# Units of 88 slots in place of 96 in the expert FFN of the second layer

## The reference, cut to what matters

```python
x = _layernorm(x).reshape(-1, 256)                       # 1024 rows
probs = softmax(x @ gate_w)                              # 64 experts
top_vals, top_idx = jax.lax.top_k(probs, 8)
rw = scatter(top_vals / sum(top_vals), top_idx)          # 1024 x 64, 8 per row
g = einsum('th,ehi->tei', x, w_gate)                     # 256 -> 96
u = einsum('th,ehi->tei', x, w_up)
h = silu(g) * u * rw[:, :, None]
out = einsum('tei,eih->th', h, w_down)                   # 96 -> 256
```

## Time and profile before

| what | value |
|---|---|
| time, median of 3 runs | 365.51 us (364.02 to 365.74) |
| the profiled execution's own time | 366.64 us |
| its span, first to last instruction | 364.9 us |
| mean granted TensorE clock | 0.894 |
| PE busy | 271.3 us (74%) |
| DVE busy | 242.4 us (66%) |
| POOL busy | 157.3 us (43%) |
| ACT busy | 148.4 us (41%) |
| moved by DMA | 89.63 MB, mean 246 GB/s |

### The profile page before, as it was taken

One profiled execution on the slowest core, in us unless ns is written; L12 is line 12 of the kernel. 1 busy time (PEld: TensorE's weight loads), 2 busy tenths in 40 slices (PEclk: granted clock), 3 DMA queues, 4 the chain that ended last, 5 costly groups with the idle time before them and its releaser, 6 DMA issues.

```text
span 364.9 us, 6915 instructions
## 1 busy us (share of the span) xinstructions
PE 271.3 (74%) x1993; PEld 225.5 (62%) x1993; DVE 242.4 (66%) x885; ACT 148.4 (41%) x427; POOL 157.3 (43%) x195
## 2 busy tenths in 40 slices
PE   4898428803775016637899999979999999998852
PEld 1334218702775015526788988968888988886741
DVE  0699999898947845435668997968677776441001
ACT  2145624430664335212444444434444444446700
POOL 4552020300242787777777100000777753337770
PEclk9999999965599555785999999999999999998988
DMA  4899999962890133349999999956999999965532
GB/s 112 297 305 320 286 348 361 332 212 61 252 272 18 70 113 110 112 166 295 372 385 384 379 282 320 345 192 175 265 327 319 331 335 336 316 203 173 170 102 73
DMA packets 46789, 89.63 MB, mean 246 GB/s; under 512 B 8384, under 2 KB 12320, under 8 KB 46752
## 3 DMA queue, kind: packets, MB, share of 16 engines
q10 hardware_dynamic: 20400, 37.95, 32.3%
q1 hardware_dynamic: 20208, 34.45, 29.6%
q0 software_dynamic: 6144, 16.79, 14.3%
HBM read 51.91 MB, written 37.26 MB: 244 GB/s over the span
## 4 chain that ended last, share of the span: by engine, by line
PE 53%; DVE 22%; POOL 11%; issue 5%; DMA 3%; ACT 2%; SPq 1%; POOLq 0%; DVEq 0%; ACTq 0%
PE psum L854 23%; PE psum L862 15%; POOL expert_rows L586 8%; DVE work L1192 6%; PE psum L842 6%; DVE top L1188 5%; PE psum L743 3%; DVE stats L1163 2%; PE psum L732 2%; PE psum L921 2%; POOL xn L645 1%; PE psum L669 1%; POOL rstd L555 1%; DVE xs L1217 1%; POOL pen L645 1%
## 5 line engine op out<-in xcount | busy, mean ns | idle before, releaser
L586 POOL DMA_INDIRECT expert_rows<-x_rows,place_at x64 | 62.7, 979 | 24.5 <-issue 24.5
L1089 ACT ACTIVATE up<-psum 96x96 f32<-96x96 f32 x128 | 31.5, 246 | 80.1 <-PE psum L854 80.1
L1474 DVE TENSOR_TENSOR up<-up,psum 96x96 f32<-96x96 f32 x128 | 32.0, 250 | 39.5 <-ACT up L1089 31.9
L619 POOL DMA_INDIRECT work<-expert_rows,gather_at x32 | 30.3, 947 | 63.5 <-issue 56.1
L1469 DVE COPY silu<-psum 128x192 f32<-128x192 f32 x128 | 45.6, 357 | 16.4 <-PE psum L842 11.4
L842 PEld LDWEIGHTS psum<-ident,gu_w 96*128 96x128 f32 x256 | 36.2, 143 | 29.3 <-DMA gu_w<-expert_rows 10.7
L842 PE MATMUL psum<-ident,gu_w 96*128 96x96 f32 x256 | 43.1, 252 | 11.8 <-DMA gu_w<-expert_rows 9.9
L854 PE MATMUL psum<-silu,wgu 128*96 128x96 f32 x448 | 49.8, 256 | 0.2 <-DVE silu L1469 0.2
L854 PEld LDWEIGHTS psum<-silu,wgu 128*96 128x96 f32 x448 | 45.2, 173 | 0.9 <-DVE silu L1469 0.5
L862 PE MATMUL psum<-proj_t,up 96*96 96x256 f32 x128 | 38.2, 380 | 0.0
L555 POOL TENSOR_TENSOR rstd<-var_eps,minus_half 128x2 f32<-128x2 f32 (+1 forms) x13 | 10.4, 798 | 46.7 <-DVE var_eps L1169 46.6
(11 more groups left out here) (240 smaller groups left out, 580.2 us busy)
## 6 DMA issues: line engine op xcount, KB each, us to landing
expert_rows<-empty_rows ACTq DMA_DIRECT2D x1, 14784.0 KB, 69.2
gu_w<-expert_rows ACTq DMA_DIRECT2D x52, 192.0 KB, 9.5
wgu<-in_L_ffn_w_gate_up SPq DMA_DIRECT2D x21, 384.0 KB, 9.6
expert_rows<-down_w ACTq DMA_DIRECT2D x32, 192.0 KB, 8.1
proj_t<-in_L_ffn_w_down SPq DMA_DIRECT2D x24, 192.0 KB, 10.4
base<-in_L_ffn_w_gate_up SPq DMA_DIRECT2D x6, 384.0 KB
adj<-in_L_ffn_w_gate_up SPq DMA_DIRECT2D x6, 384.0 KB, 5.7
gu_w<-expert_rows SPq DMA_DIRECT2D x12, 192.0 KB, 5.3
```

What stands on the lines that cost most here:

```text
L586: pool.indirect_dma_start(rows_dram, bass.IndirectOffsetOnAxis(ap=place_at[:, t, k:k + 1], axis=0), x_rows[:, t, :], None).then_inc(placed ...
L619: pool.indirect_dma_start(gathered[:, n % G_RING], None, rows_dram[0:X_OVER], bass.IndirectOffsetOnAxis(ap=gather_at[:, t, k:k + 1], axis= ...
L1089: act.activation(silu1[:, u % 2], psum[0:I1, 2 + u % 2, 0:CAP], ACT.Silu).then_inc(silu1_ready, 1)
L1474: dve.tensor_tensor(h1_t[:, u % 2], silu1[:, u % 2], psum[0:I1, 2 + u % 2, CAP:2 * CAP], ALU.mult).then_inc(h_ready, 1)
```

## The change

A unit has 88 slots in place of 96, in both phases. A pair then takes 176 rows in place of 192, the tiles of slots and outputs have 88 partitions in place of 96, the transposes and the gate and up matmuls have 88 moving columns, and the down matmul has 88 stationary columns. The constants with which DVE divides a slot number by `PAIR_ROWS` and a count by `CAP` are changed to suit. Nothing else is touched.

```diff
-CAP = 96
+CAP = 88
...
-PAIR_FACTOR = 683
-PAIR_SHIFT = 11
+PAIR_FACTOR = 745
+PAIR_SHIFT = 13
...
-link(dve.tensor_scalar(n_over_i[:, 0], n_over[:], 683.0, None, ALU.mult))
+link(dve.tensor_scalar(n_over_i[:, 0], n_over[:], 745.0, None, ALU.mult))
...
-link(dve.tensor_scalar(pick_int[:], pick_int[:], 6, None, ALU.arith_shift_right))
+link(dve.tensor_scalar(pick_int[:], pick_int[:], 4, None, ALU.arith_shift_right))
```

## The result

The changed kernel takes **397.0 us** (median of 4 runs, 395.4 to 398.09) beside 365.62 for the kernel before (4 runs, 364.02 to 365.99): a ratio of 1.0849, 95% interval 1.0806 to 1.0892. The prediction was 375.5 us with a range to 386: the direction is right, the size is not. The profiled execution has a span of 396.3 us, 31.4 above the 364.9 of before. Both profiles hold 6915 instructions: the overflow loop ran no more often than before.

The account below looks back on a forecast made before the run. It took the end to hang on pair 58's output landing, with PE and DMA both at their limit. +2 (clear) + 1 (phase 0) + 9.5 (phase 1) - 2.5 (PE) = +10 us gave 375.5 us, range 363.5 to 386.

Parts of the forecast that it names:

- Eleven engines: Transfers of 88 rows go in equal shares to 11 DMA engines, 8 rows each in place of 6.
- The clear: Zeroing the DRAM rows before the first scatter lands later, at 114 up to 125: +2 us, bounds 0 and 8.
- an engine's rate stays: In the clear, each DMA engine keeps 21 GB/s, so a third more bytes take a third more time.
- Phase 0: Unit loop, 168 to 239: slot and output transfers lag more, but PE does not stall: 0 us, bounds 0 and 9.
- 1 us left over: Of phase 0's 9 us more transfer time, spare time from 239 to 258 absorbs 8; 1 us carries on.
- the ring of eight: Slot and output buffers for eight pairs, 20.5 us, just hold phase 0's transfer lag of 20.1 us.
- Phase 1: Unit loop, 258 to 321: a third more on ACT's transfers delays pair 58's output by 9.5 us, bounds 0 and 12.
- Pair 58's output: Near the unit loop's end, its landing releases the last waiting late gather and so sets the kernel's end.
- PE: Unit loop matmuls and transposes: narrower units save 36 ns each (0 to 70), 2.5 us by 258.
- The end: POOL's last wait ends near 332 to 336, then 24 gathers follow at 1.25 us.
- A: Rival: slot and output rows spread over all 16 engines, 3 to 5 us less, 360.5 to 362.5; chance 0.14.
- B: Rival: eleven engines, but the rings hide the lag and pair 58 lands 3 us late at most, 364 to 367; chance 0.12.

Follow-up runs that it names:

- e7x: e3 with the slot loads alone moving only partitions 0 to 87 (11 engines), outputs still from 96 partitions: 371.25 us.
- e3: The kernel before with its blocks and transfers of 96 slots kept, but a unit's compute on 88 columns: 366.72 us.
- f9: e3 with slot and output transfers of partitions 0 to 79 only (16 engines), plus a small second clear on POOL's queue: 373.05 us.
- a9: The changed kernel (blocks of 176 rows) with the clear on 96 partitions and slot and output transfers of partitions 0 to 79 only: 374.17 us.
- e1: The changed kernel with only the clear put back on 96 partitions: 374.79 us.
- e7: e3 with slot and output transfers of partitions 0 to 87 only, plus a small second clear on ACT's queue behind the large one: 423.61 us.

## Why the prediction was right and wrong

*Eleven engines*: right, by the shares 0.67 and 0.75.

*The clear, taken as +2 with bounds 0 and 8; measured +22.3.* This is the step that failed, in two places. First, the sum's value: the prediction's own working ended at a landing of up to 125, 8.5 us after 116.49, and 2 was picked for lack of a row that said where in between. The upper end itself was too low, as it counted twelve weight loads where the trace has sixteen: 8 x 576 KB are 4.7 MB, 14 us an engine in place of 11, and a landing at 128. 55 and 66 partitions, which do no more than the prediction's arithmetic (11 engines, 648 or 650 pieces), put the scatter at 126 to 129: the upper end, put right, was the value. Secondly, "an engine's rate stays" did not hold: eight of the eleven engines ended 51 us after the other three, at 13 GB/s where 21 was taken, and the clear lands with the slowest. That is the other 10 to 13 us (44 and 88 against 55 and 66); they hang on the block's size, of which no row of before tells anything. The measured duration scaled by pieces would have been safer than a mean rate, as it holds the slowest engine of before: 69.2 x 648/462 = 97, a landing at 124 before any of the sixteen loads is added. It would still have missed these last 10 to 13 us.

*Phase 0, taken as 0 with bounds 0 and 9, 1 us left over; measured +7.2.* Inside the bounds. The lag was to be held by the ring of eight; what gave way first was ACT's own queue, whose issues of slot loads hold it in front of the silu. That path was not in the prediction (e7x: some 3 us are PE's waits for slots, which the ring was to prevent).

*Phase 1, taken as +9.5; measured +2.0.* The third more of ACT's transfers did not set the pace: PE is busy 63.00 of 63.00 us there, at a share of 0.90, and no transfer's issue holds ACT over 0.65 us after 270. The mechanism is there, but small. Pair 58's output, read as in the earlier trace rows, after:

```profile
350.21 0.30 ACTq L1110 DMA_DIRECT2D expert_rows<-down_w  x1
```

The gather at 355.93 starts 5.7 us after this issue, where it was 2.8 before: the output is 2.9 us later, and 1.0 us of that is made up between the first gather and this issue. The two phases together came near (10.5 less 2.5 for PE taken, 9.2 measured), but that is luck: 1 of it was taken for phase 0, which measured 7.2, and the rest for phase 1.

*PE, taken as 36 ns a unit; measured about 10.* L854 holds 85 ns with 88 moving columns: the lower bound was the value. e3 shows that this is worth nothing in the time.

*The end* went as said: 24 gathers follow the last wait, 355.93 to 385.93 is 24 x 1.25 us, 40.4 us from the wait to the end in both kernels. The wait itself is at 355.93 and not at 332 to 336. The landings of the outputs could not be compared: the profile lists none for these transfers.

*Rivals.* A fell with the shares. Its price was near all the same: 80 partitions on 16 engines (f9, a9, so with fewer bytes still) run 1.0 to 3.7 us shorter from the first scatter on than before, in one execution each, where A had 3 to 5. B fell with the clear.

## What to carry to other kernels

Before a tile's partitions are changed, ask for each DMA that touches them how its rows divide over the engines, and begin with the longest one, even if it is only a clear: scale its measured time by the pieces of each engine and look at what starts when it lands. It lands with its slowest engine, so a mean rate is too kind. A DMA that falls behind costs most where its issue stands in a compute engine's queue, in front of work that the bound engine needs. To repair such a shape, choose rows that divide well for that one transfer (here 72 or 96); cutting every transfer in two buys little.

## What was not expected of the hardware

- An issue is not always short: up to 3.52 us on ACT in e1, 1.9 to 2.9 us on SP during the clear, in the kernel before as well, and 58.25 us behind one large DMA on the same queue (e7).
- At the same number of engines and pieces, a clear in blocks of 88 or 176 rows ended 10 to 13 us later than one in blocks of 110 or 132. By the ends of the engines' parts, six or eight of the eleven took nearly twice as long as the others. Why they did is not explained.
- With 96 stationary columns a f32 matmul record of L854 follows the one before it by 85 ns, whether 96 or 88 columns move.
